# A third weight buffer, x loads on two DMA queues, an earlier first load and merged blocks in a six-layer transformer kernel

## The chip, the cores and the metric

The kernel runs on all 8 cores of one Trainium2 chip, two dies of four cores. The cores work on different sequences (2 of 16 each) and do not talk to each other. The metric is the device time of the slowest core in microseconds.

## The reference

The input x has 16 sequences of 2048 tokens with 1024 features. A first part (a recurrent attention solved by conjugate gradients, with projections and a layer norm) precedes, and is not touched by the change. The second part is six times

```
x = attn_layer(shift_tokens(x), ...) + x
x = ffn_layer(shift_tokens(x), ...) + x

attn_layer: qkv = x @ Wqkv; q, k = l2norm(q) * qs, l2norm(k) * ks; rotary; 
            softmax over a window of 256 + 256 keys, 16 heads of 64; out @ Wo
ffn_layer:  mu, var over features; xn = (x - mu) / sqrt(var + 1e-5) * g + b
            a, gate = split(xn @ W1 + b1); (a * gelu(gate)) @ W2 + b2     (2730 hidden)
```

shift_tokens delays the upper half of the features by one token. A last residual and layer norm follow.

## The kernel before

Activations lie feature-major in HBM, as 8 chunks of 128 features by 2049 columns (a zero column in front serves the shift): strA before attention, strB before the feed-forward layer (FFN). A core has 2 sequences (b), each cut into 4 tiles of 512 tokens (kk), so 8 tiles (tt) per layer. `tr_emit` runs 6 times `tr_emit_attn_layer` and `tr_emit_ffn_layer`. Each of them first loads its weights (f32 in HBM, bf16 in SBUF, by GpSimd's queue) and then emits 8 tiles. For the FFN w1 stays in SBUF, while w2 is streamed anew for each tile, in 22 pieces of 128 x 1024.

An attention tile: load x (`tr_xst`, 8 x 128 x 513 f32), cast to bf16 (line 2070), the qkv product (2091), squares and their sums over heads (2156, 2114), Ln and Exp for the reciprocal root (2163 to 2173), scaling and rotary (2187 to 2231), windowed attention, the Wo product with the residual, store to strB, and copies of the last keys and values for the next tile.

An FFN tile: load x (line 2521 on), cast (2530), sums and sums of squares (2550, 2556), the row arithmetic of the layer norm on one partition (2563 to 2585), broadcast and normalisation (2593 to 2619), the w1 product with Gelu (2637 to 2669; "w1 stage"), the w2 product (2693; "w2 stage") with all 8 PSUM banks as accumulators, the residual (2709), store to strA.

The order is set by `nc.Block()`: each block holds streams of instructions for several engines, and ends with a barrier over all of them. Inside a block engines are ordered by semaphores only. `SemScope` gives semaphores and, on leaving, adds a block in which GpSimd clears them one by one. `DmaStream` (SP: "S", 4 deep; GpSimd: "G", 8 deep) hands out DMA semaphores in turn; an issue first waits for the DMA that used the same semaphore one round before:

```
def issue(self, eng, dst, src, slow=False):
    j = self.i % self.depth
    if self.i >= self.depth:
        eng.wait_ge(self.sems[j], (self.i // self.depth) * 16)
    eng.dma_start(dst, src, ...).then_inc(self.sems[j], 16)
```

In the w2 stage one group is the 8 matmuls (one for each bank) that use one piece of w2. Semaphore u1 counts the finished groups, and GpSimd waits for it before it overwrites a buffer.

## Time and profile before

| | us |
|---|---|
| Median of 3 runs (lowest, highest) | 47055.3 (46974.9, 47211.8) |
| Profiled execution, its own time | 47048.7 |
| Its span, core 3, the slowest | 47047.2 |
| Shortest span of a core (core 4) | 46737.7 |
| Mean granted TensorE clock, cores 0 to 3 and 4 to 7 | 0.616, 0.622 of 2.4 GHz |
| Busy on core 3: TensorE matmuls, VectorE, ScalarE, GpSimd | 23288.6, 15280.7, 11069.2, 9700.0 |

All times of rows are those of core 3, from the start of its span. In the rows PE is TensorE's matmul, PEld its weight load, DVE VectorE, ACT ScalarE, POOL GpSimd, SPq the queue of SyncE; "PEq L2518" as the one who ended an idle time stands for a block's barrier. Matmuls are pipelined, so their single durations overlap. The rows themselves stand below the change.

### The profile page before, as it was taken

How to read it: one execution, taken by the hardware profiler on the slowest of the kernel's cores; microseconds unless marked ns; L12 is line 12 of the kernel's file. 1: busy time of each engine (PE TensorE's matmuls, PEld its weight loads, DVE VectorE, ACT ScalarE, POOL GpSimd, SP SyncE). 2: the span in 40 equal slices, each digit the busy share in tenths (PEclk: the TensorE clock that was granted, in tenths of full speed). 3: DMA queues.
4: the chain of work that ended last, by engine and by line, in shares of the span. 5: the costliest groups of instructions: out<-in, count | busy, mean ns of one | idle time of the engine just before them, and what ended most of it. 6: DMA issues, size and time to landing. Idle time of an engine off the chain costs nothing. (4 is left out here: it accounts for less than half of the span.)

```text
span 47047.2 us, 431097 instructions; the slowest of 8 cores (46737.7 to 47047.2 us)
## 1 busy us (share of the span) xinstructions
PE 23288.6 (50%) x100416; PEld 9488.5 (20%) x100416; DVE 15280.7 (32%) x35189; ACT 11069.2 (24%) x23857; POOL 9700.0 (21%) x10483
## 2 busy tenths in 40 slices
PE   3344444444444445555555555564556555655555
PEld 1111111111111112222222222222222222222221
DVE  3333333333333334412442144213431343124412
ACT  1122222222222213311331133212321233113310
POOL 3343343343343411100110011001110110011101
PEclk6555555555555565687667755676667666765577
DMA  1100000000000020022002200121012100210022
GB/s 47 34 1 6 6 1 6 6 1 6 6 1 6 14 55 11 13 48 42 15 11 42 49 11 11 35 43 24 15 27 43 33 11 23 41 38 11 11 49 74
DMA packets 658550, 1091.13 MB, mean 23 GB/s; under 512 B 243428, under 2 KB 260328, under 8 KB 637432
## 3 DMA queue, kind: packets, MB, share of 16 engines
q0 software_dynamic: 223312, 449.07, 6.2%
q1 hardware_dynamic: 432824, 614.46, 4.0%
q8 instruction: 954, 15.63, 0.1%
q14 instruction: 1460, 11.96, 0.1%
HBM read 1184.70 MB, written 310.64 MB: 32 GB/s over the span
## 5 line engine op out<-in xcount | busy, mean ns | idle before, releaser
L2315 PE MATMUL tr_pp<-c_identb,tr_psb 128*128 128x128 bf16 x11520 | 1768.9, 295 | 3960.2 <-DVE tr_psb L2389 3424.5
L2693 PE MATMUL tr_fw<-tr_G,tr_w 128*128 128x512 bf16 x8448 | 2390.8, 438 | 1742.3 <-DMA tr_w<-w2p 1740.0
L2091 PE MATMUL tr_pq<-tr_xb,tr_wqkv 128*128 128x512 bf16 x9216 | 2186.2, 393 | 1955.0 <-PEq L2066 1954.2
L2420 ACT COPY tr_ptb<-tr_pp 128x256 bf16<-128x256 bf16 x5760 | 1868.5, 374 | 2830.2 <-PE tr_pp L2315 2823.8
L2637 PE MATMUL tr_fg<-tr_xn,tr_w 128*128 128x512 bf16 x8448 | 2185.3, 406 | 627.7 <-PEq L195 627.7
L2244 POOL COPY tr_kprev<-tr_kp 128x256 bf16<-128x256 bf16 x384 | 134.1, 400 | 10955.5 <-DVEq L2240 10720.1
L1498 POOL TENSOR_TENSOR cg_X<-cg_X,cg_mu 128x512 bf16<-128x512 bf16 x960 | 1083.5, 1149 | 5387.3 <-DVE cg_mu L1412 5387.3
L2644 PE MATMUL tr_fg<-tr_xn,tr_w 128*128 128x512 bf16 x8448 | 2141.9, 400 | 0.0
L2408 ACT ACTIVATE tr_psb<-tr_ml,tr_mx 128x512 bf16<-128x512 f32 (+1 forms) x3072 | 2106.5, 687 | 92.5 <-DVE tr_mx L2378 72.5
L2372 DVE TENSOR_REDUCE tr_mx<-tr_ml 128x1 f32<-128x512 f32 (+1 forms) x3072 | 2003.4, 652 | 327.2 <-DVE tr_ml L2364 12.3
L265 POOL DMA_DIRECT2D tr_w<-w2p x1056 | 561.4, 532 | 7296.5 <-ACTq L2679 4158.3
L2364 DVE SCALAR_TENSOR_TENSOR tr_ml<-tr_pa,tr_mk 128x512 f32<-128x512 f32 (+1 forms) x3072 | 1993.1, 649 | 179.4 <-PE tr_pa L2301 176.5
L2315 PEld LDWEIGHTS tr_pp<-c_identb,tr_psb 128*128 128x128 bf16 x11520 | 899.8, 112 | 5155.5 <-issue 4972.8
L1363 PE MATMUL cg_pss<-cg_r,c_blk2b 128*2 128x512 bf16 x960 | 561.4, 585 | 2758.8 <-POOL cg_r L1516 2758.8
L2669 DVE SCALAR_TENSOR_TENSOR tr_G<-tr_fg,tr_bb,tr_psb 128x512 bf16<-128x512 f32 x1056 | 792.4, 750 | 3351.1 <-ACT tr_psb L2658 3351.1
L2709 DVE SCALAR_TENSOR_TENSOR tr_yst<-tr_fw,tr_bb,tr_xst 128x512 f32<-128x512 f32 x384 | 282.0, 749 | 4440.9 <-PE tr_fw L2693 4059.6
L2384 DVE RECIPROCAL tr_mx<-tr_mx 128x1 f32<-128x1 f32 x3072 | 503.3, 164 | 3722.3 <-ACT tr_psb L2408 3722.3
L2341 PE MATMUL tr_po<-tr_ptb,tr_vt 128*64 128x256 bf16 x4608 | 1273.7, 415 | 695.0 <-ACT tr_ptb L2420 695.0
L1308 PE MATMUL cg_psa<-cg_Pt,cg_Skk 128*128 128x128 bf16 x3840 | 1092.9, 285 | 1007.9 <-POOL cg_Pt L1492 771.8
L2091 PEld LDWEIGHTS tr_pq<-tr_xb,tr_wqkv 128*128 128x128 bf16 x9216 | 895.5, 100 | 3081.9 <-issue 2121.8
L2693 PEld LDWEIGHTS tr_fw<-tr_G,tr_w 128*128 128x128 bf16 x8448 | 850.3, 108 | 3281.7 <-issue 2846.2
L1385 DVE TENSOR_TENSOR cg_W<-cg_A,cg_psU 128x512 bf16<-128x512 bf16 x1920 | 1190.6, 682 | 875.3 <-PE cg_psU L1290 874.8
(341 smaller groups left out, 46839.9 us busy)
## 6 DMA issues: line engine op xcount, KB each, us to landing
tr_w<-w2p POOLq DMA_DIRECT2D x1056, 256.0 KB, 4.2
tr_xst<-strA SPq DMA_DIRECT2D x384, 256.5 KB, 3.7
tr_xst<-strB SPq DMA_DIRECT2D x384, 256.5 KB, 3.8
strB<-tr_yst SPq DMA_DIRECT2D x384, 256.0 KB, 2.8
strA<-tr_yst SPq DMA_DIRECT2D x384, 256.0 KB, 3.0
tr_w<-w1p POOLq DMA_DIRECT2D x48, 1408.0 KB, 34.3
tr_wqkv<-wqkv_t POOLq DMA_DIRECT2D x48, 768.0 KB, 19.1
cg_ktm<-kh SPq DMA_DIRECT2D x32, 512.0 KB, 5.1
```

Source lines behind the costliest of these rows:

```text
L1308: t.matmul(psa[:, po:po + 128], Skkb[:, j * NCK * CC + c * CC: j * NCK * CC + (c + 1) * CC], Pt2[:, j * T + c * CC: j * T + (c + 1) * CC], ...
L1385: v.tensor_mul(W4[:, hh * 512:(hh + 1) * 512], A4[:, hh * NCK * CC + 4 * w * CC: hh * NCK * CC + 4 * (w + 1) * CC], psU[:, hh * 512:(hh + ...
L2091: ins = t.matmul(qps[:, bank * 512:(bank + 1) * 512], wq_sb[:, kc * 3 * D + nco * 128: kc * 3 * D + (nco + 1) * 128], rhs_sh(kc), start=(k ...
L2315: ins = t.transpose(pps[:, (pos % 2) * 1024 + qt * 128: (pos % 2) * 1024 + (qt + 1) * 128], g["psb"][:, ((idx % 2) * 2 + qt) * 512 + ks * 128:
L2341: ins = t.matmul(ops[0:64, (idx % 2) * 512: (idx % 2) * 512 + 256], vsl, g["ptb"][:, (idx % 2) * 1024 + ks * 256: (idx % 2) * 1024 + (ks + ...
L2364: v.scalar_tensor_tensor(g["ml"][:, ((idx % 2) * 2 + qt) * 512: ((idx % 2) * 2 + qt) * 512 + nk], aps[:, ((2 * idx + qt) % 4) * 512: ((2 * ...
L2372: v.reduce_max(g["mx"][:, p8 + qt:p8 + qt + 1], g["ml"][:, ((idx % 2) * 2 + qt) * 512: ((idx % 2) * 2 + qt) * 512 + nk], axis=AX).then_inc ...
L2408: s.activation(g["psb"][:, ((idx % 2) * 2 + qt) * 512: ((idx % 2) * 2 + qt) * 512 + nk], g["ml"][:, ((idx % 2) * 2 + qt) * 512: ((idx % 2) ...
L2420: s.copy(g["ptb"][:, (idx % 2) * 1024 + ks * 256: (idx % 2) * 1024 + (ks + 1) * 256], pps[:, (pos % 2) * 1024:(pos % 2) * 1024 + 256]).the ...
L2637: t.matmul(gps[:, (2 * p) * 512:(2 * p + 1) * 512], w1_sb[:, kc * 2 * DH1 + hc * 128: kc * 2 * DH1 + (hc + 1) * 128], xnb[:, kc * TT:(kc + ...
L2644: ins = t.matmul(gps[:, (2 * p + 1) * 512:(2 * p + 2) * 512], w1_sb[:, kc * 2 * DH1 + DH1 + hc * 128: kc * 2 * DH1 + DH1 + (hc + 1) * 128] ...
L2693: ins = t.matmul(wps2[:, co * 512:(co + 1) * 512], w2_sb[:, (hc % 2) * D + co * 128: (hc % 2) * D + (co + 1) * 128], Gb[:, hc * TT:(hc + 1 ...
```

## The change

Five edits. (1) w2_sb has three buffers instead of two; the load of piece hc waits for group hc-3 instead of hc-2. (2) The x load of tiles 1 to 7 of each layer is split: chunks 0 to 3 are issued by SP, chunks 4 to 7 by GpSimd. (3) The x load of tile 0 of each layer is issued by SP in the block that loads the layer's weights, ahead of its small loads, and the tile waits for its ticket only. (4) The blocks of the norm's row arithmetic become one, and its square moves from GpSimd to VectorE. (5) The clamp, Ln and Exp in attention move into the block ahead of them. Edits 4 and 5 order the steps by semaphores: 3 more per tile pair (1 in attention, 2 in the FFN).

```diff
--- before.py
+++ after.py
@@ -1953,6 +1953,8 @@
             yst=mk("tr_yst", [128, 2 * TT], F32),
             zc=mk("tr_zc", [128, 1], F32),
         )
+        g["tkA"] = {}
+        g["tkB"] = {}
         with nc.Block() as blk:
             @blk.sync
             def _(sy):
@@ -2014,6 +2016,12 @@
         @blk.sync
         def _(sy):
             ld = kb.stream("S")
+            ld.wait_all(sy)
+            XB = NCH * 513
+            for c in range(NCH):
+                tk = ld.issue(sy, g["xst"][:, c * 513:(c + 1) * 513],
+                              d["strA"][0, c, :, 0:513])
+            g["tkA"][0] = tk
             ld.issue(sy, g["qsc"][:, 0:1], d["qs2"][l])
             ld.issue(sy, g["qsc"][:, 1:2], d["qs2s"][l])
             ld.issue(sy, g["qsc"][:, 2:3], d["ks2"][l])
@@ -2059,10 +2067,22 @@
     with nc.Block() as blk:
         @blk.sync
         def _(sy):
-            for c in range(NCH):
-                xs.issue(sy, g["xst"][:, c * 513:(c + 1) * 513],
-                         d["strA"][b, c, :, kk * TT:kk * TT + 513])
-            xs.wait_all(sy)
+            if tt > 0:
+                for c in range(4):
+                    xs.issue(sy, g["xst"][:, c * 513:(c + 1) * 513],
+                             d["strA"][b, c, :, kk * TT:kk * TT + 513])
+                xs.wait_all(sy)
+            else:
+                xs.wait(sy, g["tkA"][0])
+
+        @blk.gpsimd
+        def _(gp):
+            if tt > 0:
+                xg = kb.stream("G", depth=8)
+                for c in range(4, NCH):
+                    xg.issue(gp, g["xst"][:, c * 513:(c + 1) * 513],
+                             d["strA"][b, c, :, kk * TT:kk * TT + 513])
+                xg.wait_all(gp)
     with nc.Block() as blk:
         @blk.scalar
         def _(s):
@@ -2078,7 +2098,7 @@
           nc.psum_tensor(f"tr_pss{l}{tt}", [16, 1024], PS) as sps,
           nc.psum_tensor(f"tr_ptr{l}{tt}", [128, 2048],
                          mybir.dt.bfloat16) as tps,
-          SemScope(kb, 6, "trQ") as (s1, s2, s3, s4, s5, s6)):
+          SemScope(kb, 7, "trQ") as (s1, s2, s3, s4, s5, s6, s7)):
         with nc.Block() as blk:
             @blk.tensor
             def _(t):
@@ -2131,6 +2151,12 @@
                         dst = g["kp"][:, (i - 16) * TT:(i - 15) * TT]
                     s.copy(dst, qps[:, bank * 512:(bank + 1) * 512]
                            ).then_inc(s2, 1)
+                s.wait_ge(s7, 2)
+                s.activation(g["ssq"][:, :], g["ssq"][:, :], AF.Ln
+                             ).then_inc(s7, 1)
+                s.wait_ge(s7, 3)
+                s.activation(g["rstd"][:, :], g["ssq"][:, :], AF.Exp,
+                             scale=-0.5)
 
             @blk.vector
             def _(v):
@@ -2155,23 +2181,12 @@
                            g["kp"][:, (i % 8) * TT:(i % 8 + 1) * TT])
                     v.tensor_mul(g["sq"][:, (i % 2) * TT:(i % 2 + 1) * TT],
                                  src, src).then_inc(s5, 1)
-
-        with nc.Block() as blk:
-            @blk.vector
-            def _(v):
                 for qk in range(2):
+                    v.wait_ge(s6, 16)
                     v.tensor_scalar(g["ssq"][:, qk * TT:(qk + 1) * TT],
                                     sps[:, qk * 512:(qk + 1) * 512],
-                                    1e-24, None, AluOpType.max)
-        with nc.Block() as blk:
-            @blk.scalar
-            def _(s):
-                s.activation(g["ssq"][:, :], g["ssq"][:, :], AF.Ln)
-        with nc.Block() as blk:
-            @blk.scalar
-            def _(s):
-                s.activation(g["rstd"][:, :], g["ssq"][:, :], AF.Exp,
-                             scale=-0.5)
+                                    1e-24, None, AluOpType.max
+                                    ).then_inc(s7, 1)
 
     for qk, srcb, dstb, ctab, stab in (
             (0, g["qp"], g["qp"], "csql", "ssql"),
@@ -2478,7 +2493,7 @@
     wl_ = kb.stream("G", depth=8)
 
     with (nc.sbuf_tensor(f"tr_w1{l}", [128, NCH * 2 * DH1], BF16) as w1_sb,
-          nc.sbuf_tensor(f"tr_w2{l}", [128, 2 * D], BF16) as w2_sb,
+          nc.sbuf_tensor(f"tr_w2{l}", [128, 3 * D], BF16) as w2_sb,
           nc.sbuf_tensor(f"tr_bb{l}", [128, 2 * NHC + 3 * NCH], F32) as bb_sb,
           nc.sbuf_tensor(f"tr_xn{l}", [128, NCH * TT], BF16) as xnb,
           nc.sbuf_tensor(f"tr_G{l}", [128, NHC * TT], BF16) as Gb,
@@ -2494,6 +2509,11 @@
             @blk.sync
             def _(sy):
                 ld = kb.stream("S")
+                ld.wait_all(sy)
+                for c in range(NCH):
+                    tk = ld.issue(sy, g["xst"][:, c * 513:(c + 1) * 513],
+                                  d["strB"][0, c, :, 0:513])
+                g["tkB"][0] = tk
                 ld.issue(sy, bb_sb[:, 0:2 * NHC], d["b1c"][l])
                 ld.issue(sy, bb_sb[:, 2 * NHC:2 * NHC + NCH], d["lng"][l])
                 ld.issue(sy, bb_sb[:, 2 * NHC + NCH:2 * NHC + 2 * NCH],
@@ -2518,10 +2538,22 @@
     with nc.Block() as blk:
         @blk.sync
         def _(sy):
-            for c in range(NCH):
-                xs.issue(sy, g["xst"][:, c * 513:(c + 1) * 513],
-                         d["strB"][b, c, :, kk * TT:kk * TT + 513])
-            xs.wait_all(sy)
+            if tt > 0:
+                for c in range(4):
+                    xs.issue(sy, g["xst"][:, c * 513:(c + 1) * 513],
+                             d["strB"][b, c, :, kk * TT:kk * TT + 513])
+                xs.wait_all(sy)
+            else:
+                xs.wait(sy, g["tkB"][0])
+
+        @blk.gpsimd
+        def _(gp):
+            if tt > 0:
+                xg = kb.stream("G", depth=8)
+                for c in range(4, NCH):
+                    xg.issue(gp, g["xst"][:, c * 513:(c + 1) * 513],
+                             d["strB"][b, c, :, kk * TT:kk * TT + 513])
+                xg.wait_all(gp)
     with nc.Block() as blk:
         @blk.scalar
         def _(s):
@@ -2532,7 +2564,7 @@
 
     with (nc.psum_tensor(f"tr_f1{l}{tt}", [1, 512], PS) as sp1,
           nc.psum_tensor(f"tr_f2{l}{tt}", [1, 512], PS) as sp2,
-          SemScope(kb, 2, "trF") as (q1, q2)):
+          SemScope(kb, 4, "trF") as (q1, q2, f1, f2)):
         with nc.Block() as blk:
             @blk.vector
             def _(v):
@@ -2561,27 +2593,22 @@
             @blk.vector
             def _(v):
                 v.tensor_scalar(rowb[0:1, 0:TT], sp1[0:1, :], 1.0 / D, None,
-                                AluOpType.mult)
+                                AluOpType.mult).then_inc(f1, 1)
                 v.tensor_scalar(rowb[0:1, TT:2 * TT], sp2[0:1, :], 1.0 / D,
-                                None, AluOpType.mult)
-        with nc.Block() as blk:
-            @blk.gpsimd
-            def _(gp):
-                gp.tensor_mul(rowb[0:1, 2 * TT:3 * TT], rowb[0:1, 0:TT],
-                              rowb[0:1, 0:TT])
-        with nc.Block() as blk:
-            @blk.vector
-            def _(v):
+                                None, AluOpType.mult).then_inc(f1, 1)
+                v.wait_ge(f1, 2)
+                v.tensor_mul(rowb[0:1, 2 * TT:3 * TT], rowb[0:1, 0:TT],
+                             rowb[0:1, 0:TT]).then_inc(f1, 1)
+                v.wait_ge(f1, 3)
                 v.tensor_sub(rowb[0:1, TT:2 * TT], rowb[0:1, TT:2 * TT],
-                             rowb[0:1, 2 * TT:3 * TT])
-        with nc.Block() as blk:
+                             rowb[0:1, 2 * TT:3 * TT]).then_inc(f1, 1)
+
             @blk.scalar
             def _(s):
+                s.wait_ge(f1, 4)
                 s.activation(rowb[0:1, TT:2 * TT], rowb[0:1, TT:2 * TT],
-                             AF.Ln, bias=P["epsc"][0:1, 1:2])
-        with nc.Block() as blk:
-            @blk.scalar
-            def _(s):
+                             AF.Ln, bias=P["epsc"][0:1, 1:2]).then_inc(f2, 1)
+                s.wait_ge(f2, 1)
                 s.activation(rowb[0:1, TT:2 * TT], rowb[0:1, TT:2 * TT],
                              AF.Exp, scale=-0.5)
 
@@ -2680,9 +2707,9 @@
             @blk.gpsimd
             def _(gp):
                 for hc in range(NHC):
-                    if hc >= 2:
-                        gp.wait_ge(u1, hc - 1)
-                    w2s.issue(gp, w2_sb[:, (hc % 2) * D:(hc % 2 + 1) * D],
+                    if hc >= 3:
+                        gp.wait_ge(u1, hc - 2)
+                    w2s.issue(gp, w2_sb[:, (hc % 3) * D:(hc % 3 + 1) * D],
                               d["w2p"][l, hc])
 
             @blk.tensor
@@ -2692,8 +2719,8 @@
                     for co in range(NCH):
                         ins = t.matmul(
                             wps2[:, co * 512:(co + 1) * 512],
-                            w2_sb[:, (hc % 2) * D + co * 128:
-                                  (hc % 2) * D + (co + 1) * 128],
+                            w2_sb[:, (hc % 3) * D + co * 128:
+                                  (hc % 3) * D + (co + 1) * 128],
                             Gb[:, hc * TT:(hc + 1) * TT],
                             start=(hc == 0), stop=(hc == NHC - 1),
                             skip_group_check=True)
```

## Rows read from the trace of the kernel before

**Rows 1.** Groups of instructions: matmuls of the w2 product (busy, mean ns, idle before).
```profile
L2693 PE MATMUL tr_fw<-tr_G,tr_w 128*128 128x512 bf16 x8448 | 2390.8, 438 | 1742.3 <-DMA tr_w<-w2p 1740.0
```

**Rows 2.** Line 2693: duration of its matmuls, ns, least, median, most.
```profile
L2693 PE MATMUL tr_fw<-tr_G,tr_w x8448: 376/379/634, 20216.3 to 46636.9; 128*128 128x512 bf16 x197
```

**Rows 3.** Timeline of one w2 stage: start, length, what, idle before.
```profile
20216.30 5.49 PE L2693 MATMUL tr_fw<-tr_G,tr_w 128*128 128x512 bf16 x16 [7.44 <-DMA tr_w<-w2p]
...
20217.11 0.15 PEld L2693 LDWEIGHTS tr_fw<-tr_G,tr_w 128*128 128x128 bf16 x1 [0.28 <-issue]
20217.53 0.15 PEld L2693 LDWEIGHTS tr_fw<-tr_G,tr_w 128*128 128x128 bf16 x1 [0.28 <-issue]
...
20224.97 1.89 PE L2693 MATMUL tr_fw<-tr_G,tr_w 128*128 128x512 bf16 x8 [3.18 <-DMA tr_w<-w2p]
...
20248.20 0.53 POOL L265 DMA_DIRECT2D tr_w<-w2p  x1 [2.70 <-PE tr_fw L2693]
...
20249.05 1.89 PE L2693 MATMUL tr_fw<-tr_G,tr_w 128*128 128x512 bf16 x8 [1.46 <-DMA tr_w<-w2p]
20251.54 0.53 POOL L265 DMA_DIRECT2D tr_w<-w2p  x1 [2.81 <-PE tr_fw L2693]
...
20252.68 1.89 PE L2693 MATMUL tr_fw<-tr_G,tr_w 128*128 128x512 bf16 x8 [1.75 <-DMA tr_w<-w2p]
...
20289.13 1.89 PE L2693 MATMUL tr_fw<-tr_G,tr_w 128*128 128x512 bf16 x8 [0.62 <-DMA tr_w<-w2p]
```

**Rows 4.** Windows: a w1 stage, a w2 stage, another w1 stage, a w1 load.
```profile
core 3: us, PE busy (x) PEld busy (x) DVE busy (x) ACT busy (x) POOL busy (x), PEclk, DMA share, GB/s
20130.70:20211.50 80.80, 78.12 (x352) 34.88 (x352) 16.50 (x22) 16.40 (x23) 0.00 (x0) 0.97 0.00 1
20216.30:20291.00 74.70, 43.20 (x176) 16.09 (x176) 0.00 (x0) 0.00 (x0) 10.55 (x20) 0.97 0.50 71
40357.00:40450.00 93.00, 92.98 (x352) 38.41 (x352) 15.76 (x21) 15.72 (x22) 0.00 (x0) 0.81 0.00 1
44732.60:44789.20 56.60, 0.00 (x0) 0.00 (x0) 0.00 (x0) 0.00 (x0) 4.31 (x8) 0.50 0.99 204
```

**Rows 5.** Timeline at two x loads, and landing times of the second.
```profile
20309.65 6.47 SPq L265 DMA_DIRECT2D tr_xst<-strB  x8
20320.46 1.28 ACT L2530 ACT_TABLE_LOAD   x1 [110.82 <-PEq L2518]
...
44362.24 5.87 SPq L265 DMA_DIRECT2D tr_xst<-strA  x8
44371.73 1.28 ACT L2070 ACT_TABLE_LOAD   x1 [39.17 <-PEq L2059]
...
DMA to landing us min/median/max: 3.3/3.6/3.8
```

**Rows 6.** Timeline of the norm's row arithmetic.
```profile
20334.33 0.67 DVE L2565 TENSOR_SCALAR tr_row<-tr_f 1x512 f32<-1x512 f32 x1
20335.29 1.03 POOL L2570 TENSOR_TENSOR tr_row<-tr_row 1x512 f32<-1x512 f32 x1 [49.71 <-DVEq L2567]
20336.65 0.68 DVE L2575 TENSOR_TENSOR tr_row<-tr_row 1x512 f32<-1x512 f32 x1 [1.65 <-PEq L2567]
20337.60 1.28 ACT L2580 ACT_TABLE_LOAD   x1 [11.59 <-PEq L2572]
```

**Rows 7.** Timeline around Ln and Exp in attention.
```profile
22109.73 1.28 DVE L2163 TENSOR_SCALAR tr_ssq<-tr_pss 16x512 f32<-16x512 f32 x2 [0.85 <-PEq L2082]
...
22113.88 1.28 ACT L2173 ACT_TABLE_LOAD   x1 [0.26 <-PEq L2166]
22115.17 1.05 ACT L2173 ACTIVATE tr_rstd<-tr_ssq 16x1024 bf16<-16x1024 f32 x1
...
22117.19 0.58 PE L2187 MATMUL tr_pr<-tr_rstd,c_selT8b 16*128 16x512 bf16 x1 [7.78 <-PEq L195]
22117.88 0.69 DVE L2205 TENSOR_TENSOR tr_qp<-tr_qp,tr_pr 128x512 bf16<-128x512 bf16 x1 [6.87 <-PE tr_pr L2187]
```

## The prediction

> **What bounds the kernel now.** I read the cores and the busy times first, then the list of instruction groups for lines that the diff touches, largest waits first; then timelines and windows of their stages. In the w2 product (line 2693) TensorE is busy 2390.8 us and idle 1742.3 us, and 1740.0 us of that idle time ended with the landing of a w2 load [rows 1]. This is the only large wait that the diff touches. Its 48 runs (6 layers, 8 tiles) each begin after 7.44 us of idleness that lies before the first matmul [rows 3], so one w2 stage lasts (2390.8 + 1742.3 - 48 x 7.44)/48 = 78.7 us, of which 49.8 us are matmuls.
>
> The timeline of one stage shows the mechanism. A group of eight matmuls takes 1.89 us, GpSimd issues the next load 0.60 us after the group ends (20249.05 + 1.89 to 20251.54), and the group that consumes a load starts 4.48 us after its issue (20248.20 to 20252.68) [rows 3]. One buffer's cycle is thus 1.89 + 0.60 + 4.48 = 6.97 us. With two buffers a group can start every 3.49 us; the stage's own pace is (20289.13 - 20224.97)/19 = 3.38 us, a cycle of 6.76 us [rows 3]. I use 6.9 us. The stage is bound by a round trip and not by TensorE or bandwidth: the 16 DMA engines are busy half of it (0.50), while a block that does nothing but load w1 keeps them at 0.99 [rows 4].
>
> The other edits sit in places where all engines wait for one: the x load at the head of each tile [rows 5], the layer norm's row arithmetic [rows 6], the Ln and Exp in attention [rows 7]. There everything lies on the path, since the blocks end in a barrier.
>
> **Third w2 buffer.** It removes nothing and adds no load; load hc now waits for group hc-3. The steady step becomes a third of the cycle, 6.9/3 = 2.30 us, wherever TensorE is faster than that. At the full 2.4 GHz it is: a group is 1.89 us. At 1.2 GHz it is not: weight loads start 0.42 us apart (20217.11, 20217.53) [rows 3], so a group takes 8 x 0.427 = 3.41 us and TensorE itself sets the pace. The matmuls of this line last 379 ns at the median and up to 634 ns [rows 2], with a mean of 438 ns [rows 1]; (438 - 379)/(634 - 379) = 23% of them at the low level is my estimate. The mean step is then 0.77 x 2.30 + 0.23 x 3.41 = 2.56 us. The start: three loads are issued together, the first three groups run without a wait, and the fourth starts when its load is there: 3.5 us for the first group (cold after the idle stretch) + 0.60 + 4.48 = 8.6 us. The stage: 8.6 + 18 x 2.56 + 1.9 = 56.6 us, against 78.7. The same reckoning for two buffers (8.6 us to the third group, a step of 3.45 or 4.3, mean 3.65, 19 times, and 1.9) gives 79.8, within 1.1 us of the measured mean. Term: 22.1 x 48 = **-1061 us**.
>
> Bounds: if TensorE has the full clock throughout, 8.6 + 18 x 2.30 + 1.9 = 51.9 us, -1286 us. If three loads in flight delay each other by one more load's transfer: the w1 block moves 8 x 1408 KB in 56.6 us, so 256 KB in 1.29 us [rows 4]; the cycle is 8.2 us, the step 0.77 x 2.73 + 0.23 x 3.41 = 2.89 us, the stage 62.5 us, -778 us. I take the first value: one load occupies the DMA engines for 0.50 x 3.38 = 1.7 us [rows 3, 4], and at a step of 2.30 us that is 0.73 of the time, below the 0.99 they reach. The group before needs 1.7 us only, so transfers need not overlap.
>
> **x load on two queues (84 of 96 tiles).** Now SP issues all eight, four in flight: the issuing lasts 6.47 us, because the fifth waits for the first to land, and ScalarE starts 10.8 us after the first issue; in another tile, of attention, 9.5 us [rows 5]. Between these two for all 96 tiles: 10.2 us. After: SP issues four, GpSimd four at about 0.53 us [rows 3], all within 2 us. The first lands after 3.3 us [rows 5]; the rest follow at what the engines move, 8 x 1408 KB of bf16, read as 8 x 2816 KB of f32, in 56.6 us [rows 4], hence 0.65 us for 256.5 KB: the last lands at 3.3 + 7 x 0.65 = 7.8 us, and 0.8 us pass to ScalarE's start. 10.2 - 8.6 = 1.6 us, times 84 = **-134 us**. Bounds: 0, if a GpSimd-issued load is as much later as the stall was long, and 4.1 us (-344 us), if the last lands 3.7 us after its issue at 1.6 us and bandwidth does not matter.
> The trace says that the stall comes from the depth of four, not from the engines: the DMA share at full load is 0.99 and the issuing has a hole in it [rows 4, 5]. The Trainium skill, DMA: Bandwidth & Descriptors, section "Issuing engines are not separate DMA queues", says that issuing from several engines saves only the sequencer's issue time, usually small beside the transfer. By that rule alone this term would be near 0 and the sum 134 us smaller; no row here shows a load issued from both.
>
> **First x load of a layer moved into the weight block (12 of 96).** SP's eight issues with their stalls now run beside GpSimd's weight loads. On SP only four small loads are queued behind them, and the block lasts 56.6 us [rows 4], so nobody waits for these. The tile's own wait falls from 10.2 to about 0.4 us: -9.8 x 12 = -118 us. But the block that covers it is itself bound by DMA (0.99 [rows 4]), so 8 x 0.65 = 5.2 us of transfers lengthen it: +62 us. Net **-56 us**; bounds 0 and -118.
>
> **Merged blocks.** Norm: now two scale operations, 0.29 us, GpSimd's square 1.03, 0.33, the subtraction 0.68, 0.27 to the table load [rows 6], and 0.26 between Ln and Exp (as in attention [rows 7]). After: the square on VectorE at 0.68 (the subtraction's row, same shape), and hand-overs by semaphore at 0.11 us, as 22117.77 to 22117.88 [rows 7]. 2.86 - (4 x 0.11 + 2 x 0.68) = 1.06 us, x 48 = **-50 us**. Attention: three boundaries of about 0.27 us (0.26 before the table load of line 2173) become 0.11 [rows 7]: 0.5 x 48 = **-23 us**. The table loads stay: they stand behind the wait in both forms. Bounds of both: 0 and -90 us, the latter if boundaries cost twice what these rows show. New semaphores: one and two more to clear per tile, 144 in all. From Exp's end to the next matmul are 0.97 us for two boundaries and six clears [rows 7]; less 2 x 0.29 leaves 0.065 us a clear: **+9 us**.
>
> **Sum.** -1061 - 134 - 56 - 50 - 23 + 9 = -1315 us. The profiled execution took 47048.7 us (span 47047.2 and 1.5 around it), 7 us under the median of the runs. 47048.7 - 1315 = 45734, say **45,730 us**.
>
> **Rivals.**
> *Loads in flight delay each other.* For: four constant tables and w1 queue behind each other already. Against: the share of 0.50 [rows 4]. w2 gives 778 instead of 1061: 46,020 us. Chance 0.11.
> *TensorE's clock falls because it works more densely.* In one w1 stage the granted clock is 0.97 and the stage takes 80.8 us; in another 0.81, 93.0 us, TensorE busy throughout in both [rows 4]. That is 1.95 GHz, between the two levels. If all 48 w1 stages went that way, at most +12.2 x 48 = 586 us; w2 itself would hardly notice, as 8 matmuls at 0.81 take 2.1 us, less than the step. 45,734 + 586 = 46,320 us. The Trainium skill, TensorE: Matmul & The Clock Gate, Part 1, has a peak-current limiter that takes a whole die to 13/16 once a third core runs dense matmuls. By that rule the 0.81 should become commoner when w2 grows denser; the row shows the level, not its cause. Against the full price: many stages pay it already. Chance 0.10.
> *The third buffer does nothing*, because something else holds GpSimd's issue back. Then -254 us remain: 46,795. Against: its issue follows the end of the group by 0.60 us each time [rows 3]. Chance 0.02.
> *Slower than before.* One mechanism: with three loads in flight each takes much longer from issue to use, L instead of 4.48 us. With a mean group of 2.26 us (2390.8/1056) [rows 1] the stage takes (3.5 + 0.60 + L) + 18 x (2.26 + 0.60 + L)/3 + 1.9 = 23.2 + 7L. That is the old 78.7 us at L = 7.9, and with the 254 us of the other terms (5.3 a tile) the kernel breaks even at L = 8.7 us. At L = 11 us the stage takes 100.2 us and the kernel 47048.7 + 21.5 x 48 - 254 = 47,830 us. For it: no row shows all cores loading with three in flight. Against: loads at full rate take 1.29 us per 256 KB [rows 4]. Chance 0.03.
>
> **How the numbers follow.** Forecast 0.72, the rest 0.02 for mixtures beyond these. Its own range is 45,450 (full clock in w2) to 45,900. The range for 8 in 10 takes in most of the first two rivals and the better bounds: 45,400 to 46,250. A measurement of this kernel tells about 0.5% (235 us) from no change. Faster by more: forecast, first two rivals and a part of the third, 0.95; within 0.5% 0.02; slower 0.03.
>
> **What would show it.** The w2 stage near 57 us, groups 2.3 us apart, idle time before line 2693 down from 1742 to about 680 us, DMA share in it 0.7. ScalarE 8.6 us after the first x issue. First tile of a layer: 0.4 us; weight blocks 5 us longer. Norm chain 1.1 us shorter, its square on VectorE. I am wrong if landings of w2 take much over 4.5 us, if w1 stages sit at 0.81, or if x loads from GpSimd land last.

## The result, and the profile after

The changed kernel takes 45597.9 us (median of 9 runs, 45484.2 to 45973.7), the kernel before beside it 47055.0 us (median of 10). The ratio is 0.9705, 95% interval 0.968 to 0.973. The forecast of 45,730 us was 132 us too high, and the range held. The profiled execution took 45783.2 us, 185 above the median and 1265.6 less than that of before. The prediction's sum starts from the profiled execution of before and said 1315 less, so against the profiled executions it took off 49 us too much.

The cores' own spans and clocks, the slowest core and the middle of each die:

```profile
core 4: 45781.6 us, clock 0.608
...
die 0 (median of its cores): 45491.1 us, clock 0.620
die 1 (median of its cores): 45755.6 us, clock 0.611
```

The page of the same execution, w2 and w1 groups and the DMA issues with their median time to landing:

```profile
L2720 PE MATMUL tr_fw<-tr_G,tr_w 128*128 128x512 bf16 x8268 | 2253.9, 424 | 741.1 <-DMA tr_w<-w2p 723.2
L2664 PE MATMUL tr_fg<-tr_xn,tr_w 128*128 128x512 bf16 x8280 | 2258.1, 419 | 640.6 <-PEq L195 629.4
...
tr_w<-w2p POOLq DMA_DIRECT2D x1056, 256.0 KB, 4.6
...
tr_xst<-strB SPq DMA_DIRECT2D x216, 256.5 KB, 4.1
...
tr_xst<-strB POOLq DMA_DIRECT2D x168, 256.5 KB, 6.3
```

The first row answers to [rows 1]: idle time before w2 matmuls fell from 1742.3 (core 3) to 741.1 us (core 4), of which 48 x 6.94 us lie before a stage's first matmul. The stage now lasts (2253.9 + 741.1 - 48 x 6.94)/48 = 55.5 us on this core. (Some matmul records are missing in this trace, hence x8268.) The last rows are new: of the x loads, those that GpSimd issues take 2.2 us longer to land than those of SP, in attention 2.5 us (6.4 and 3.9).

The timeline of one w2 stage on core 4, beside [rows 3]:

```profile
20186.17 1.66 POOL L265 DMA_DIRECT2D tr_w<-w2p  x3 [81.62 <-ACTq L2706]
20190.24 7.40 PE L2720 MATMUL tr_fw<-tr_G,tr_w 128*128 128x512 bf16 x23 [6.94 <-DMA tr_w<-w2p]
...
20217.64 0.53 POOL L265 DMA_DIRECT2D tr_w<-w2p  x1 [2.14 <-PE tr_fw L2720]
20217.73 1.89 PE L2720 MATMUL tr_fw<-tr_G,tr_w 128*128 128x512 bf16 x8 [0.69 <-DMA tr_w<-w2p]
...
20219.96 1.89 PE L2720 MATMUL tr_fw<-tr_G,tr_w 128*128 128x512 bf16 x8 [0.34 <-DMA tr_w<-w2p]
20220.22 0.53 POOL L265 DMA_DIRECT2D tr_w<-w2p  x1 [2.05 <-PE tr_fw L2720]
...
20222.52 1.89 PE L2720 MATMUL tr_fw<-tr_G,tr_w 128*128 128x512 bf16 x8 [0.67 <-DMA tr_w<-w2p]
```

Three loads go out at once. The group of 20217.73 ends at 20219.62 and GpSimd issues 0.60 us later, as before. The load issued at 20217.64 is used three groups on, at 20222.52, after 4.88 us (4.48 before). The cycle is 1.89 + 0.60 + 4.88 = 7.37 us, a third of it 2.46 us, and the gaps before the groups shrank from 1.5 to about 0.6 us.

The window of this stage (columns as in [rows 4]) has a DMA share of 0.70 against 0.50:

```profile
20190.20:20243.20 53.00, 42.42 (x172) 16.42 (x176) 0.00 (x0) 0.00 (x0) 10.03 (x19) 0.96 0.70 101
```

The timeline of the next FFN tile's head, beside [rows 5, 6]:

```profile
20265.41 1.75 SPq L265 DMA_DIRECT2D tr_xst<-strB  x4
20265.87 2.13 POOL L265 DMA_DIRECT2D tr_xst<-strB  x4 [28.62 <-PEq L2538]
20275.29 1.28 ACT L2562 ACT_TABLE_LOAD   x1 [91.21 <-PEq L2538]
...
20289.83 0.67 DVE L2597 TENSOR_SCALAR tr_row<-tr_f 1x512 f32<-1x512 f32 x1
20290.60 0.68 DVE L2600 TENSOR_TENSOR tr_row<-tr_row 1x512 f32<-1x512 f32 x1
20291.38 0.68 DVE L2603 TENSOR_TENSOR tr_row<-tr_row 1x512 f32<-1x512 f32 x1
20292.15 1.28 ACT L2609 ACT_TABLE_LOAD   x1 [11.31 <-DVE tr_row L2603]
20293.44 0.72 ACT L2609 ACTIVATE tr_row<-tr_row,c_epsc 1x512 f32<-1x512 f32 x1
20294.26 0.63 ACT L2612 ACTIVATE tr_row<-tr_row 1x512 f32<-1x512 f32 x1
```

Two things are to be seen. The issuing no longer stalls (1.75 and 2.13 us instead of 6.47), yet ScalarE starts 9.9 us after the first issue, where 8.6 were forecast. And Exp (line 2612) follows Ln after 0.10 us with no table load between them. In attention both loads are gone: Ln and Exp follow each other on ScalarE like this,

```profile
22247.02 1.05 ACT L2155 ACTIVATE tr_ssq<-tr_ssq 16x1024 f32<-16x1024 f32 x1 [8.83 <-DVE tr_ssq L2186]
22248.17 1.05 ACT L2158 ACTIVATE tr_rstd<-tr_ssq 16x1024 bf16<-16x1024 f32 x1
```

Before, the instruction groups of ScalarE had four table loads at these places, after one; 3 x 48 = 144 loads are gone. The two in attention, before (those of the norm, lines 2580 and 2585, look alike):

```profile
L2169 ACT ACT_TABLE_LOAD x48 | 61.6, 1283 | 445.9 <-PEq L2159 445.9
L2173 ACT ACT_TABLE_LOAD x48 | 61.6, 1283 | 12.3 <-PEq L2166 12.3
```

After:

```profile
L2152 ACT ACT_TABLE_LOAD x48 | 61.6, 1283 | 188.4 <-PE tr_pq L2111 188.4
...
L2609 ACT ACT_TABLE_LOAD x48 | 61.6, 1283 | 534.6 <-DVE tr_row L2603 534.6
```

The load of line 2152 stood in front of the copies before too (line 2132); now it serves Ln and Exp behind them as well.

To see where the time went I summed the length of every stage over its 48 tiles (or its layers) in the profiled execution, as a mean over the 8 cores. The other columns are changes against before, for this kernel and for four of the experiments below. "Storing" is the Wo product with its stores, the end of the attention tile and the FFN's residual with its stores; stages that are left out moved by 22 us at most.

| us | before | after | e1: buffer | e2: merged | e11: both | e12: no split |
|---|---|---|---|---|---|---|
| w2 stage | 3675 | -1042 | -1034 | -44 | -1017 | -1050 |
| Ln/Exp and norm rows | 815 | -259 | +3 | -259 | -259 | -259 |
| x loads inside layers | 1163 | -18 | +46 | +6 | +40 | +36 |
| switch to the next layer | 909 | +10 | +79 | +19 | +73 | +28 |
| storing | 2039 | +48 | +141 | +54 | +143 | +120 |
| qkv product | 2946 | -2 | +26 | -6 | +74 | +35 |
| w1 stage | 3897 | -6 | -14 | -21 | +85 | -103 |
| whole span | 46896 | -1285 | -723 | -249 | -859 | -1201 |

### The profile page after: what moved, and what is told of

The parts are those of the page before. It is cut to its first block and busy times, and to the rows that moved or that the text cites. A ratio compares the mean times of both kernels' runs of the same rounds, so it can differ in the third digit from the quotient of the medians.

```text
span 45781.6 us, 427515 instructions; the slowest of 8 cores (45463.2 to 45781.6 us)
## 1 busy us (share of the span) xinstructions
PE 23249.3 (51%) x99510; PEld 9512.0 (21%) x100416; DVE 15323.3 (33%) x35237; ACT 10881.5 (24%) x23713; POOL 9831.8 (21%) x10771
## 5 line engine op out<-in xcount | busy, mean ns | idle before, releaser
L2720 PE MATMUL tr_fw<-tr_G,tr_w 128*128 128x512 bf16 x8268 | 2253.9, 424 | 741.1 <-DMA tr_w<-w2p 723.2
L2664 PE MATMUL tr_fg<-tr_xn,tr_w 128*128 128x512 bf16 x8280 | 2258.1, 419 | 640.6 <-PEq L195 629.4
L2671 PE MATMUL tr_fg<-tr_xn,tr_w 128*128 128x512 bf16 x8274 | 2204.0, 411 | 12.4
L2685 ACT ACTIVATE tr_psb<-tr_fg,tr_bb 128x512 bf16<-128x512 f32 x1056 | 725.5, 687 | 3126.1 <-PE tr_fg L2671 3125.5
L1456 ACT CAST cg_Apb<-cg_psa 128x512 bf16<-128x512 f32 x960 | 561.7, 585 | 3712.1 <-DVE cg_tm L1394 3675.5
## 6 DMA issues: line engine op xcount, KB each, us to landing
tr_xst<-strA SPq DMA_DIRECT2D x216, 256.5 KB, 3.9
tr_xst<-strB SPq DMA_DIRECT2D x216, 256.5 KB, 4.1
tr_xst<-strA POOLq DMA_DIRECT2D x168, 256.5 KB, 6.4
tr_xst<-strB POOLq DMA_DIRECT2D x168, 256.5 KB, 6.3
```

What stands on the lines that cost most here:

```text
L2664: t.matmul(gps[:, (2 * p) * 512:(2 * p + 1) * 512], w1_sb[:, kc * 2 * DH1 + hc * 128: kc * 2 * DH1 + (hc + 1) * 128], xnb[:, kc * TT:(kc + ...
L2671: ins = t.matmul(gps[:, (2 * p + 1) * 512:(2 * p + 2) * 512], w1_sb[:, kc * 2 * DH1 + DH1 + hc * 128: kc * 2 * DH1 + DH1 + (hc + 1) * 128] ...
L2720: ins = t.matmul(wps2[:, co * 512:(co + 1) * 512], w2_sb[:, (hc % 3) * D + co * 128: (hc % 3) * D + (co + 1) * 128], Gb[:, hc * TT:(hc + 1 ...
```

## The experiments

Each starts from the kernel before or from the changed one, or from an earlier experiment, as said. The time before is that of runs on the same chip. Three chips were used, so times of different experiments are best compared by their ratios.

**e1: the third buffer alone.** From before; only edit 1.

```diff
-                    if hc >= 2:
-                        gp.wait_ge(u1, hc - 1)
+                    if hc >= 3:
+                        gp.wait_ge(u1, hc - 2)
```

> The kernel before with the third w2 buffer alone. Round-trip theory: the w2 stage falls from 78.7 to about 55 us (in the changed kernel it was 54.1 to 55.7 us on the eight cores), the idle time ahead of the w2 matmuls from 1742 to about 740 us, and the kernel by about 1040 us (ratio 0.978). Rival, that the w2 gain in the changed kernel came with its other edits (a colder or warmer clock, earlier x loads): the w2 stage stays above 60 us here.

Measured: 46328.8 us, ratio 0.9843 (0.9819 to 0.9866), against 47068.6. The w2 stage gave 1034 us, as in the full change, but the whole gave 723: the stages that move activations became longer (table above). The w2 row of its page; the landing's median is 4.7 us:

```profile
L2693 PE MATMUL tr_fw<-tr_G,tr_w 128*128 128x512 bf16 x8268 | 2183.4, 413 | 826.4 <-DMA tr_w<-w2p 810.4
```

**e2: the merged blocks alone.** From before; edits 4 and 5, of which ScalarE's part in attention is shown.

```diff
+                s.wait_ge(s7, 2)
+                s.activation(g["ssq"][:, :], g["ssq"][:, :], AF.Ln
+                             ).then_inc(s7, 1)
+                s.wait_ge(s7, 3)
+                s.activation(g["rstd"][:, :], g["ssq"][:, :], AF.Exp,
+                             scale=-0.5)
```

> The kernel before with the merged blocks of norm and attention alone, nothing else. In the changed kernel three activation table loads per tile pair are gone (144 of 1283 ns). Table theory: both merged chains lose what they lost there, 110 us in the norm rows and 148 us in the Ln and Exp step, 259 us in all (ratio 0.9945), and the 144 table loads are gone here too. Rival, my prediction's step (hand-overs of 0.11 instead of 0.27 us, table loads kept): 73 us in all (0.9985).

Measured: 46805.6 us, 0.9956 (0.9939 to 0.9973). The Ln/Exp step became 149 us shorter and the norm rows 111 us, the same as in the full change, and 3.5 times the 73 us of the prediction.

**e3: the x split alone.** From before; edit 2, tile 0 left as it was.

```diff
+            if tt > 0:
+                xg = kb.stream("G", depth=8)
+                for c in range(4, NCH):
+                    xg.issue(gp, g["xst"][:, c * 513:(c + 1) * 513], ...)
+                xg.wait_all(gp)
```

> The kernel before with the x loads of tiles 1 to 7 split over SP and GpSimd, and nothing else. Theory now, from the changed kernel's trace: loads issued by GpSimd land last, about 9.1 us after the first issue, so the x load step stays within 0.3 us of the 10.2 us it took; the kernel does not move (ratio 0.999 to 1.001). Rival, the prediction's step: the last lands at 7.8 us, 134 us gained (0.997).

Measured: 47036.9 us, 0.9987 (0.9964 to 1.0009). The x loads inside layers became 32 us shorter, 0.4 us each, where 134 were forecast. Over all these loads and all cores the last piece lands 8.96 us after the first issue, against 9.83 before.

**e4: the earlier first load alone.** From before; edit 3.

```diff
+            ld.wait_all(sy)
+            for c in range(8):
+                tk = ld.issue(sy, g["xst"][:, c * 513:(c + 1) * 513],
+                              d["strA"][0, c, :, 0:513])
```

> The kernel before with only the first x load of each layer moved into the weight block. Theory now: the weight block grows by about 11 us (in the changed kernel 60.6 to 71.7 us for w1 and 46.3 to 57.3 us for Wqkv and Wo, mean of the cores), a little more than the 9.8 us that the first tile saves, so the kernel does not move (ratio 0.9995 to 1.001). Rival, the prediction's step: the block grows by 5.2 us and 56 us are gained (0.9988); that can be told apart by the length of the blocks alone.

Measured: 47056.6 us, 0.9990 (0.9967 to 1.0014). Blocks that load w1 grew from 60.6 to 69.1 us (mean of all), those that load the attention weights from 46.3 to 54.7: 8.5 us each, nearly all of the 9.8 us that the tile saves. The layer switches as a whole became 22 us shorter, where 56 were forecast. The timeline of a last layer's block on core 3, which issues w1 0.24 us after x begins, with the landing times of w1 (9.8/31.3/52.8 us in the same block before):

```profile
44514.70 21.83 SPq L265 DMA_DIRECT2D tr_xst<-strB  x8
...
DMA to landing us min/median/max: 12.9/36.9/59.8
```

The last w1 piece lands 7.0 us later. In the w1 blocks the last of SP's small loads now lands 0.5 us after the last piece of w1, so 0.5 us of the 8.5 are theirs.

**e5: Ln and Exp in one block each, and nothing else.** From before; clamp, square and subtraction stay in blocks of their own. This tells the table loads from the barriers.

```diff
-                s.activation(g["ssq"][:, :], g["ssq"][:, :], AF.Ln)
-        with nc.Block() as blk:
-            @blk.scalar
-            def _(s):
+                s.activation(g["ssq"][:, :], g["ssq"][:, :], AF.Ln
+                             ).then_inc(s7, 1)
+                s.wait_ge(s7, 1)
                 s.activation(g["rstd"][:, :], g["ssq"][:, :], AF.Exp,
                              scale=-0.5)
```

> The kernel before with only this: Ln and Exp of a tile stand in one block instead of two, in the norm and in attention, with a semaphore between them. Table theory (a table of ScalarE that serves all functions of a block is loaded once in that block): one load of 1283 ns and most of a boundary go, twice per tile pair; the Ln and Exp step of attention falls by about 1.45 us a tile (376 to 306 us in sum), the norm rows by 1.45 us (439 to 370 us), 140 us in all. Rival, that the loads went because the Exp follows by semaphore or because the clamp on VectorE stands in the same block: no load goes, 15 us in all.

Measured in one execution: the two steps became 67 and 68 us shorter, 1.40 us a tile, and one load stands where two stood:

```profile
L2169 ACT ACT_TABLE_LOAD x48 | 61.6, 1283 | 450.2 <-PEq L2159 450.2
...
L2172 ACT ACTIVATE tr_rstd<-tr_ssq 16x1024 bf16<-16x1024 f32 x48 | 50.7, 1057 | 4.9 <-ACT tr_ssq L2169 0.4
```

1.28 us for the load and 0.15 for a barrier (0.26) that became a semaphore (0.11), less 0.065 for clearing it, make 1.37 us. The loads carry nearly all of it. The whole run (46903.5 us, one execution) is no measurement of so small a gain.

**e6: SP's stream eight deep.** From before: the stall of the fifth issue is taken away without a second queue. (GpSimd's stream is eight deep already; the stores, which SP issues too, get the depth as well.)

```diff
-            self.streams[tag] = DmaStream(self, tag, depth)
+            self.streams[tag] = DmaStream(self, tag, 8)
```

> The kernel before with SP's stream 8 deep instead of 4, all x loads still on SP. If the hole in SP's issuing is what the x load step pays (the prediction's step, whose failure is then GpSimd's loads landing late): the last x load lands at about 7.8 us, the step falls from 10.2 to 8.6 us in all 96 tiles, 150 us in all (0.997). Rival, that 2.1 MB of x at about 0.75 us per 256.5 KB behind a first landing of 3.5 us is the bound whoever issues: the step stays at 9.9 to 10.3 us and the kernel does not move.

Measured: 47026.9 us against 47219.1, 0.9971 (0.9953 to 0.9989). The x loads inside layers changed by 12 us together; of the profiled execution's 132 us some 102 lie in the w1 stages, where no work was changed. In one tile of core 4 ScalarE starts 10.2 us after the first issue, though the issuing takes 4.14 us only:

```profile
20311.34 4.14 SPq L265 DMA_DIRECT2D tr_xst<-strB  x8
20321.56 1.28 ACT L2530 ACT_TABLE_LOAD   x1 [113.26 <-PEq L2518]
...
DMA to landing us min/median/max: 3.7/5.9/6.2
```

Over all tiles but the first of a layer, and all cores, the issuing shrank from 6.25 to 3.99 us, while the last landing after the first issue moved from 9.83 to 9.39 us and ScalarE's start from 10.26 to 9.91. The stall cost little: of 2.3 us that the issuing became shorter some 0.4 arrive, since loads issued earlier take longer to land. ScalarE's 0.35 us are 29 us in 84 tiles, and 17 of them went into a longer wait between the last work and the first issue.

**e7: four buffers.** From the changed kernel; the norm's row buffer, a quarter of which is unused, shrinks to make room.

```diff
+          nc.sbuf_tensor(f"tr_w2{l}", [128, 4 * D], BF16) as w2_sb,
+          nc.sbuf_tensor(f"tr_row{l}", [1, 3 * TT], F32) as rowb):
+                    if hc >= 4:
+                        gp.wait_ge(u1, hc - 3)
```

> The changed kernel with four w2 buffers instead of three (and the norm's row buffer cut to the three quarters that are used, to make room). Round-trip theory: a quarter of the 7 us cycle is 1.75 us, about a group at full clock (1.73 us back to back), so TensorE sets the pace: the w2 stage falls from 55 to 43 to 46 us, 450 us in all. Rival, transfers: the landing time grew from 4.2 to 4.6 us with the third buffer; if loads already delay each other, the step stays above 2.1 us, the stage above 50 us, and the landing time grows to 6 us or more.

Measured: 45400.7 us against 47219.1, 0.9638 (0.9605 to 0.9671). The w2 stage lasts 45.2 us (mean of all) against 54.9 with three buffers and 76.6 with two. TensorE's own 22 groups of 1.89 us are 41.6 us of that, so little is left to a fifth. Landing takes 5.0 us now (page, core 5):

```profile
L2720 PE MATMUL tr_fw<-tr_G,tr_w 128*128 128x512 bf16 x8448 | 2121.7, 415 | 460.0 <-DMA tr_w<-w2p 456.8
...
tr_w<-w2p POOLq DMA_DIRECT2D x1056, 256.0 KB, 5.0
```

**e8: half of the first load moved.** From before; chunks 0 to 3 in the weight block, 4 to 7 in the tile. It tells a constant cost of the move from one for each chunk.

```diff
+            for c in range(4):
+                tk = ld.issue(sy, g["xst"][:, c * 513:(c + 1) * 513],
+                              d["strA"][0, c, :, 0:513])
```

> The kernel before with only half of the first x load of each layer (4 of 8 chunks) moved into the weight block. With all eight the blocks grew by 8.5 us (60.6 to 69.1 and 46.3 to 54.7 us, mean of the cores). If the growth is the price of transfers, 1.06 us per chunk: half is 4.2 us. If most of it is a fixed price (a queue that is restarted, SP's small loads that now land after the weights): more than 6 us of the 8.5 remain.

Measured in one execution: w1 blocks of 65.9 us and attention blocks of 51.7, so +5.3 and +5.4 for four chunks, against +8.5 for eight. The cost grows with the chunks, though not in proportion. In the last layer, where the fastest w1 block of before lasted 56.7 us, the fastest lasts 61.0 with four and 63.2 with eight. For all eight that is 0.81 us a chunk, where the forecast had 0.65. But the first four cost 4.3 us and the other four 2.2, so a part of some 2 us may not grow with the chunks; what it is stays open. The time of the one run, 47085.8 us, differs from before (47219.1) by less than such a run can tell.

**e9: the first four w2 loads issued during the w1 stage.** From e7.

```diff
+            @blk.gpsimd
+            def _(gp):
+                for hc in range(4):
+                    w2s.issue(gp, w2_sb[:, hc * D:(hc + 1) * D],
+                              d["w2p"][l, hc])
```

> The kernel with four w2 buffers, and the first four pieces of w2 loaded during the w1 stage, when GpSimd and the DMA engines idle. Now 7.2 us pass from the last w1 matmul to the first of w2, of which about 4.5 are issue and landing. Theory: 7.2 falls to 2 to 2.5 us, and the w2 stage begins warmer: 230 to 330 us in all. Rival, that loads during the w1 stage disturb it (weights are read by TensorE at the same time): the w1 stage grows by 2 us or more a tile, 100 us given back.

Measured: 45026.3 us against 47204.0, 0.9543 (0.9512 to 0.9574). Against e7 the gap between the two products fell by 219 us, from 7.2 to 2.6 us a tile, and the w2 stage by 82 us. The rival (loads that disturb the w1 stage) doesn't show: that stage became 42 us shorter, no more than the clock moves it.

**e10: x loads inside the block that uses them.** From e9; the separate load and cast blocks are gone, SP issues eight deep, ScalarE casts each chunk as it lands, TensorE starts on it at once. Edits 2 and 3 are taken back.

```diff
+            @blk.scalar
+            def _(s):
+                for c in range(NCH):
+                    xs.wait(s, x_base + c + 1)
+                    s.copy(g["xbt"][:, c * 513:(c + 1) * 513],
+                           g["xst"][:, c * 513:(c + 1) * 513]).then_inc(s8, 1)
```

> The kernel with early w2 loads, and in addition: x loads and casts stand in the block that uses them, all x loads on SP with 8 in flight, ScalarE casts each chunk when it has landed, TensorE and VectorE start on it; the moved first load is taken out. The x load is bound by its transfers (8 to 9.5 us whoever issues); what can be saved is what stood behind it. Theory: cast 4.6 us and a table load of 1.28 us in attention, and 5 us of cast plus 6 us of sums in the FFN tile go, about 16 us a tile pair, 750 us beyond the early w2 kernel. Rival, that ScalarE's copies and VectorE's squares slow each other or the loads: under 400 us.

Measured: 44044.8 us against 47204.0, 0.9336 (0.9305 to 0.9366), the fastest of all. Against before, attention's cast gave 182 us and the FFN's cast and statistics 250; the x load steps gave 268 and 263, as far as a load's time can still be told from the work above it. The qkv product, which now starts on the first chunk, became longer instead (by 88 us from its first to its last matmul). Beyond e9 the cores gained 954 us in the mean, where 750 were expected; which of the edits taken together here brought how much was not tried. The w2 group of its trace:

```profile
L2695 PE MATMUL tr_fw<-tr_G,tr_w 128*128 128x512 bf16 x8268 | 2065.6, 410 | 211.9 <-PEq L195 128.1 <-DMA tr_w<-w2p 67.2 <-issue 0.7
```

Of TensorE's 1742 idle microseconds before w2 matmuls [rows 1] 212 are left, 67 of them ended by a landing.

**e11: third buffer and merged blocks,** without either x edit (from before; the diffs of e1 and e2 together).

> The kernel before with the third w2 buffer and the merged blocks, without the split x loads and the moved first load. Alone these two gave 723 and 249 us (mean of the cores); the third buffer alone took 1034 us out of the w2 stage but gave 310 back in stages that move x and results, in a trace in which two cores of a pair stay within 20 us of each other. If split and move are worth nothing and the giving back is a matter of how the pairs happen to stand: about the changed kernel's 1285 us, within 150. If split or move keeps the pairs apart and is worth 300 us so: about 970 us here.

Measured: 46078.0 us against 47204.0, 0.9762 (0.9725 to 0.9798).

**e12: the changed kernel without the split.** Edit 2 taken back; SP issues all eight for tiles 1 to 7.

```diff
-                for c in range(4):
+                for c in range(NCH):
                     xs.issue(sy, g["xst"][:, c * 513:(c + 1) * 513], ...)
```

> The changed kernel with all x loads back on SP, the rest kept. Alone, the split gave 77 us and the moved first load 45 us (mean of the cores, both mostly clock); but the kernel without both (third buffer and merged blocks only) stands at 46,078 us, 480 us above the changed one at 45,598. If the split is what matters in company: 45,950 to 46,150 us here. If the moved first load is: 45,550 to 45,700 us. If each gives a part, in between. In the slower cases the two cores of a pair should again stand within 20 us of each other in most tiles, and results and x take longer to move.

Measured: 45884.3 us against 47170.6, 0.9735 (0.9708 to 0.9763). From e11 over this to the changed kernel the ratio goes 0.9762, 0.9735, 0.9705. The first step lies inside the intervals, the second just outside (0.9705 against 0.9708 to 0.9763), though the two intervals overlap. The two together are 0.0057, about 270 us, though the two x edits alone measured 0.9987 and 0.9990, each with 1 in its interval. The time lies between the ranges that were expected for "the split matters" and "the moved load matters", so each seems to give a part.

## Why the prediction was right, and where its steps were not

**Third w2 buffer: right, in mechanism and size.** Forecast -1061 us and a stage of 56.6 us; measured -1042 us (mean of the cores) and 54.1 to 55.7 us. The issue still follows a group's end by 0.60 us, the cycle is divided by three (after) and by four (e7), until TensorE takes over at 45.2 us. Two inputs were off in opposite directions: the cycle grew to 7.37 us, a third of it 2.46 us where 2.30 were forecast, but the mean step is about (54.9 - 8.6 - 1.9)/18 = 2.47 us where 2.56 were forecast, since it kept 23% of the matmuls at the low level (on core 3 some 15% of the w2 matmuls started 0.43 us after the one before them, and now 5% do). Of the rival "loads in flight delay each other" a part came true: from issue to landing the median went to 4.6 us with three and 5.0 with four in flight, 0.4 and 0.8 us more than the 4.2 of before, and not a whole transfer of 1.29 us. The DMA share of 0.70 against the forecast 0.73 fits. That "the third buffer does nothing" and that it costs more than it brings are ruled out by e1 (0.9843).

**"The table loads stay: they stand behind the wait in both forms": the step that failed.** Merging took out 144 loads of 1283 ns, 185 us. Put these back in and the forecast's barriers are right: norm (110.6 - 61.6)/48 = 1.02 us a tile against 1.06 forecast, attention (148.5 - 2 x 61.6)/48 = 0.53 against 0.5. e5 isolates one load in each place: 67 and 68 us. My bound of 90 us for both terms left the loads out as well; the measured 259 lay far outside it. The rows for it were in the trace: [rows 6, 7] end at a table load, and the ScalarE groups above list two for each Ln and Exp pair that lies in two blocks. I read the load as the price of the function. In the kernel before, each of the nine blocks of a tile pair in which ScalarE works has one load ahead of its first function (nine lines of 48 loads), so the load is the price of a set that is chosen anew for each block. The Trainium skill, ScalarE: Activation LUTs, section "Table sets: the hidden batching unit", says that ln and then exp need one load because one set holds both. e5 and the changed kernel agree: one load with both in a block, or none where the copies ahead have the fitting set already. Before, in two blocks, there were two.

**x load on two queues: -134 us forecast, 32 measured alone.** The failed step is "the last lands at 7.8 us". Over the 84 loads of a core and all cores, the eight pieces land at these mean times after the first issue, in us:

| | 1st | 2nd | 3rd | 4th | 5th | 6th | 7th | 8th | ScalarE starts |
|---|---|---|---|---|---|---|---|---|---|
| before | 3.65 | 4.39 | 5.18 | 5.86 | 7.49 | 8.35 | 9.13 | 9.83 | 10.26 |
| after | 3.77 | 4.69 | 5.73 | 6.51 | 7.36 | 8.38 | 8.64 | 9.09 | 9.97 |
| e6, eight deep | 3.64 | 4.45 | 5.44 | 6.35 | 7.40 | 8.09 | 8.75 | 9.39 | 9.91 |

The hole in the issuing shows before, between the 4th and the 5th landing (1.63 us). After, it is gone, but the pieces follow each other at (9.09 - 3.77)/7 = 0.76 us where 0.65 were forecast, and the first lands at 3.77 us, not 3.3; that makes 9.1 us instead of 7.8. Most of what filling the hole gave is lost again by slower landings ahead of it. And of the 0.74 us by which the last piece lands earlier only 0.29 reach ScalarE, which starts 0.88 us after the last landing, against 0.43 before. The forecast had the 0.8 us right for after, but set them against a start of before in which this step was half as long. The rate of 0.65 us for 256.5 KB was taken from a load that narrows f32 to bf16, while x stays f32; whether that makes the difference was not tried. In five of six tiles a load issued by GpSimd is the last to land, but SP's last comes only 0.4 us ahead of it (8.62 and 9.02 us), and with all eight on SP (e6) the last is no earlier. So the transfers bind here, and not the engine that issues. e4 has a like price beside other traffic (5.2 us forecast for eight pieces, 6.5 measured in the last layer, 8.5 over all layers). The Trainium skill, DMA: Bandwidth & Descriptors, section "Issuing engines are not separate DMA queues", gave near 0 for this term, and e3 (0.9987, interval over 1) agrees with it.

**Earlier first load: -56 us forecast, -22 measured in the switches (e4).** The cover was itself bound by DMA, as the prediction said, but the price was 8.5 us and not 5.2, so that it eats nearly all of the 9.8. Half a microsecond of it in the w1 blocks is the small loads, for which, by the prediction, nobody waits.

**The sum.** In the full change the x loads and the layer switches together moved by 8 us, where 190 were forecast: 182 too generous. The merges gave 259 where 73 were forecast: 186 too small. That these cancel is why the sum came within 4%, and no merit of the steps.

**What the third buffer gives back.** e1 lost 310 us between the w2 stage (-1034) and the whole (-723), 265 of them in the x loads, the layer switches and the storing. These were not changed, and the prediction had no term for them. In the full change the same stages lost 40 us. The trace suggests where it comes from. Take cores 0 and 1, 2 and 3, and so on, as pairs; all cores run through the same stages, shifted in time. Before, core 1 reaches its x loads tens of us after core 0; here, on core 0 of before:

```profile
40023.87 5.88 SPq L265 DMA_DIRECT2D tr_xst<-strB  x8
```

and core 1 of before, 101 us later, with ScalarE's start:

```profile
40124.46 5.71 SPq L265 DMA_DIRECT2D tr_xst<-strB  x8
40134.06 1.28 ACT L2530 ACT_TABLE_LOAD   x1 [109.22 <-PEq L2518]
```

In e1 the same load on core 0,

```profile
39348.57 5.88 SPq L265 DMA_DIRECT2D tr_xst<-strB  x8
```

is followed by core 1's after 15 us, and ScalarE of core 1 starts 10.9 us after the first issue, where it took 9.6 us in before:

```profile
39363.45 6.37 SPq L265 DMA_DIRECT2D tr_xst<-strB  x8
39374.35 1.28 ACT L2530 ACT_TABLE_LOAD   x1 [93.84 <-PEq L2518]
```

Sorted by the distance of a pair, the stretch from the last w2 matmul to the next tile's cast (results stored, x loaded), in us, with the number of cases:

| distance of the pair, us | under 10 | 10 to 20 | 20 to 40 | over 40 |
|---|---|---|---|---|
| before | 32.4 (14) | 31.0 (11) | 30.1 (23) | 29.5 (120) |
| e1, third buffer | 32.8 (65) | 32.2 (83) | 31.1 (20) | none |
| e11, and merged blocks | 33.2 (67) | 32.2 (55) | 31.0 (29) | 29.7 (17) |
| e12, no split | 33.1 (35) | 32.2 (70) | 31.3 (13) | 30.5 (50) |
| after | 32.6 (23) | 30.9 (37) | 29.9 (76) | 29.1 (32) |

In each kernel the stretch is 2.6 to 3.5 us longer under 10 us than over 40 (1.7 us longer than at 20 to 40 in e1), and e1 and e11 keep their pairs close most of the time. With both x edits the pairs lie further apart and the stretch is shorter at each distance than in e11 and e12; so the x edits are worth something in company (0.9762 to 0.9705) that they are not alone. Cores of one die that are no pair show nothing of the kind before and after: sorted by the distance of cores 0 and 2, 1 and 3, 4 and 6, 5 and 7, the stretch of before is 29.3 us under 10 us (3 cases) and 30.0 over 40, that of the changed kernel 30.0 (14 cases) and 30.5. In e12, where more than two cores often stand close, 1.3 us remain (32.5 and 31.2). The blocks that load weights, which e1 leaves as they were, lengthened there as well, by 7.0 us for w1 and 4.8 for attention (mean of all); these twelve are most of the 79 us of the switches. All this is a correlation over five kernels. A pair held apart or together on purpose was not tried, and why e1 keeps its pairs together stays open.

**The clock rival: no price in the mean, half of it on the slowest core.** In the w1 stages a core spends part of its time at a granted clock of 0.81. Before, cores 0 to 3 have this in 25 to 34% of the stage and cores 4 to 7 in 4 to 12%; after, 0 to 6% and 26 to 54%. The w1 rows show it: core 2 of the changed kernel has a mean matmul of 390 ns,

```profile
L2664 PE MATMUL tr_fg<-tr_xn,tr_w 128*128 128x512 bf16 x8280 | 2056.5, 390 | 637.8 <-PEq L195 629.2
```

core 4 one of 419 ns (the second row of the page above). Over all cores the w1 stages changed by 6 us: cores 0 to 3 gained 211 and cores 4 to 7 lost 200. The slow level moved to the other die. Core 4, which sets the time now, paid 309 of the rival's 586 us (its w1 stages took 3840 us before and take 4149): its own span fell by 956 us only, from 46737.7 to 45781.6. The slowest core of before, core 3, fell by 1553. In the mean of all cores, in which these moves cancel, the span fell by 1285 us, near the forecast's 1315. That the slowest core of before and the slowest of after differ by about as much (1266) is luck as far as the clock goes. What sends the level to one die or the other was not tried.

## What to carry to other kernels

A stream of loads bound by a round trip (issue, landing, use, release) is sped up by buffers in proportion, until the consumer's own pace: take the cycle from one timeline, divide, compare with the busy time of a group. Count what a block's head repeats, table loads above all, before you price merging blocks by their barriers. A hole in the issuing is a cost only if the transfer behind it has finished: put more in flight (e6) before you believe in a second queue. And once the obvious stall is gone, look at the blocks that only load: letting the consumer start on the first piece, with its load and cast blocks gone (e10), brought far more than any other way of issuing.
